# Differential attention between two expert layers: values split over four places of a batch, merge and xn two tiles apart, difference ahead of xn's remainder, the second map's factor on GpSimd

## The reference

```python
x = x + 0.5 * ffn(layernorm(x))      # 8 experts, top 2, hidden 512, then a layer norm of its own
x = x + attn(layernorm(x))
x = x + 0.5 * ffn(layernorm(x))

def attn(x):                          # scale = 128 ** -0.25
    a1 = softmax((x Wq1) (x Wk1)^T * scale)
    a2 = softmax((x Wq2) (x Wk2)^T * scale)
    diff = a1 - lam_full * a2         # lam_full: one number from four vectors
    out = diff @ (x Wv)
    return out / sqrt(mean(out ** 2) + 1e-5) * 0.2
```

## Time and profile before

| | |
|---|---|
| median of 3 runs | 728.55 us (727.17 to 728.67) |
| the profiled execution's own time | 725.22 us |
| its span | 723.5 us |
| mean granted TensorE clock | 0.911 |
| busy in the span: PE, DVE, ACT, POOL | 575.7, 517.6, 413.1, 335.3 us |
| busy from 256 to 502 us (attention): PE, DVE, ACT, POOL | 206.89, 211.63, 162.94, 102.02 us of 246.00 |

### The profile page before, as it was taken

The page is one execution under the profiler, slowest core; times in us unless marked ns, Lnnn a source line. Parts: engine busy times, 40 slices in busy tenths (PEclk is TensorE's granted clock), DMA queues, the critical chain, the costliest instruction groups (busy, mean ns, idle before and its releaser), DMA issues.

```text
span 723.5 us, 16279 instructions
## 1 busy us (share of the span) xinstructions
PE 575.7 (80%) x3864; PEld 500.8 (69%) x3864; DVE 517.6 (72%) x1672; ACT 413.1 (57%) x1103; POOL 335.3 (46%) x394
## 2 busy tenths in 40 slices
PE   1745399999799877897988789776999997999800
PEld 1734399999798856566675657654689897998800
DVE  5645657866578689799789967967266874688747
ACT  3354156666365638657767676565376563777621
POOL 6357035430546303533652164273377677456513
PEclk9965589999999999999999899898899998999955
DMA  8512134422443200000010000020313232521051
GB/s 272 154 45 78 44 86 115 113 63 76 118 106 84 56 1 15 23 22 1 26 34 2 0 30 31 0 75 18 71 54 96 77 88 75 193 75 44 26 174 58
DMA packets 53675, 49.17 MB, mean 68 GB/s; under 512 B 9862, under 2 KB 45874, under 8 KB 53072
## 3 DMA queue, kind: packets, MB, share of 16 engines
q1 hardware_dynamic: 44736, 31.25, 15.7%
q0 software_dynamic: 8640, 16.87, 7.5%
q10 hardware_dynamic: 208, 0.02, 0.0%
HBM read 25.99 MB, written 23.02 MB: 68 GB/s over the span
## 4 chain that ended last, share of the span: by engine, by line
PE 51%; DVE 25%; issue 8%; ACT 7%; POOL 6%; DMA 2%; DVEq 0%; ACTq 0%; POOLq 0%; SPq 0%
PE banks L847 18%; PE banks L857 17%; DVE nb L1419 5%; POOL zb L438 4%; PE banks L926 3%; PE banks L824 2%; PE banks L839 2%; DVE scratch L1430 2%; PE banks L780 2%; PE banks L782 1%; PE banks L781 1%; DVE st_r L1072 1%; PE banks L815 1%; DVE st_x L1072 1%; ACT rowbuf L535 1%
## 5 line engine op out<-in xcount | busy, mean ns | idle before, releaser
L847 PE MATMUL banks<-scratch 128*128 128x128 f32 x1248 | 171.5, 282 | 9.8 <-DVE scratch L1210 6.5
L857 PE MATMUL banks<-blocks,scratch 128*128 x1248 | 167.3, 278 | 0.4 <-ACT scratch L585 0.3
L847 PEld LDWEIGHTS banks<-scratch 128*128 128x128 f32 x1248 | 155.7, 196 | 15.2 <-issue 8.8
L857 PEld LDWEIGHTS banks<-blocks,scratch 128*128 128x128 f32 x1248 | 154.2, 194 | 0.7 <-issue 0.7
L1217 DVE TENSOR_SCALAR scratch<-banks,blocks 128x128 f32<-128x128 f32 x312 | 95.1, 346 | 46.7 <-PE banks L847 45.9
L427 POOL DMA_INDIRECT rows<-rowbuf,slot x96 | 96.3, 1003 | 46.4 <-issue 38.8
L572 ACT ACTIVATE scratch<-banks 128x128 f32<-128x128 f32 x156 | 43.2, 277 | 122.9 <-PE banks L839 116.1
L641 ACT ACTIVATE scratch<-banks,nb 128x1024 f32<-128x1024 f32 x64 | 71.2, 1114 | 68.3 <-DVE nb L1419 68.2
L585 ACT ACTIVATE scratch<-banks,blocks 128x128 f32<-128x128 f32 x312 | 97.7, 363 | 17.4 <-PE banks L847 15.9
L449 POOL DMA_INDIRECT results<-scratch x78 | 78.0, 1000 | 46.2 <-DVE scratch L1225 26.9
L438 POOL DMA_INDIRECT zb<-yrows,slot x64 | 67.2, 1049 | 62.1 <-DMA yrows<-scratch 25.3
(11 more groups left out here) (180 smaller groups left out, 876.8 us busy)
## 6 DMA issues: line engine op xcount, KB each, us to landing
scratch<-rows SPq DMA_DIRECT2D x156, 64.5 KB, 1.9
yrows<-scratch SPq DMA_DIRECT2D x78, 64.0 KB, 1.7
rows<-padrows SPq DMA_DIRECT2D x34, 64.5 KB
x<-in_L_attn_x_dram SPq DMA_DIRECT2D x4, 512.0 KB, 6.0
scratch<-in_L_ffn_W_dram SPq DMA_DIRECT2D x1, 2048.0 KB, 20.2
out_dram<-x SPq DMA_DIRECT2D x4, 512.0 KB, 5.9
rows<-rowbuf,slot POOLq DMA_INDIRECT x96
results<-scratch POOLq DMA_INDIRECT x78, 2.3
```

Source lines behind the costliest of these rows:

```text
L847: ins = pe.matmul(hT_at(T, c), staged(T, c), xT_of(T), start=True, stop=True)
L857: ins = pe.matmul(y_at(T), hT_of(T, c), blocks[:, W2_AT + c * D:][:, bass.ds(at, D)], start=(c == 0), stop=(c == FC - 1))
```

## The change

Nothing is computed otherwise than before, except that `1 / l2` is now a power of -1 on POOL. The edits are:

1. The factor `cc` moves from DVE (two instructions in each of 32 differences) to POOL: `ratio(b, i)` waits for both exponentials of tile i, takes `l2 ** -1`, and multiplies by `l1` and `-lambda`. DVE's `difference` now waits for `cc_ready`. To fit `ratio` in, POOL's gathers and scatters are cut into runs of 2 to 4 between the tiles.
2. `values` of a batch stand at four places: the first group's halves at tile 6 and behind `turn_xn`, the second group's halves at tiles 1 and 2 of the next batch; `multiply_Wv` of it moves to tile 3. The last batch keeps its places.
3. At the joint, PE has `values`' half and one `turn_rows` ahead of `multiply_M`, and `multiply_Wv` and the other `turn_rows` behind it; ACT's `o_copy` and a `copy_tgtT` move behind the last tile.
4. DVE's `merge_add` is at tile 3 and `x_stats` of xn stays at tile 5; `add_values` and its `x_stats` move from tile 3 to 4 (batches 1 and 2), `place` from tile 4 to 6 (batch 2). On ACT, `normalise` of `sum_r`, `make_rows` and `make_xn` are each done in one piece, no longer in two.
5. On DVE `difference(6)` is ahead of `xnT_rest`.

```diff
@@ -177,6 +177,7 @@
...
         found_rows = sem("found_rows")
+        cc_ready = sem("cc_ready")
         hT_first, w1_first, w1_rest = sem("hT_first"), sem("w1_first"), sem("w1_rest")
...
@@ -281,6 +282,10 @@
...
             return 0 if b == BATCHES - 1 else 2
+
+        def place_tile(b):
+
+            return 2 if b == BATCHES - 1 else 6
...
@@ -475,29 +481,37 @@
...
+            def ratio(b, i):
+
+                c = slice(i, i + 1)
+                wait_apart(pool, (p_ready, 2 * (TB * b + i) + 2))
+                steps.then(pool.tensor_tensor(cc[:, c], l2[:, c], minus[:, :], ALU.pow))
+                pool.tensor_scalar(cc[:, c], cc[:, c], l1[:, c], nlam[:, 0:1], ALU.mult, ALU.mult).then_inc(cc_ready, 1)
+
             n = BATCHES + 2
...
                 last, after = b > 0, b < BATCHES - 1
-                if b == BATCHES - 1:
-                    scatter(1, b - 3, range(10, PAIRS))
-                if after:
-                    rstd(n)
-                    n += 1
-                if last:
-                    value_scale(b - 1, 1)
-                    rstd(n)
-                    n += 1
-                if after:
-                    if b < 2:
-                        gather(b + 2, range(4))
-                    rstd(n)
-                    n += 1
-                if b < 2:
-                    gather(b + 2, range(4, PAIRS))
-                if b == 2:
-                    scatter(1, b - 2, range(10))
-                if b == BATCHES - 1:
-                    scatter(1, b - 2)
+                for i in range(TB):
+                    ratio(b, i)
+                    if after and i == 1:
+                        rstd(n)
+                        n += 1
+                    if last and i == 2 + after:
+                        value_scale(b - 1, 1)
+                    if last and i == 3 + after:
+                        rstd(n)
+                        n += 1
+                    if after and i == 5:
+                        rstd(n)
+                        n += 1
+                    if b < 2 and 1 <= i:
+                        gather(b + 2, range(16 * (i - 1) // 7, 16 * i // 7))
+                    if b == 2 and i >= 6:
+                        scatter(1, 0, range(3 * (i - 6), 3 * (i - 5)))
+                    if b == 3 and i < 3:
+                        scatter(1, 0, ((6, 7, 8), (9, 10, 11), (12, 13, 14, 15))[i])
+                    if b == 3 and i >= 4:
+                        scatter(1, 1, range(4 * (i - 4), 4 * (i - 3)))
                 value_scale(b, 0)
...
@@ -650,43 +664,40 @@
...
                             act.wait_ge(y_written[r], sent(SLOTS, r))
-                    if last and i == 2:
+                    if last and not after and i == 2:
                         o_copy(b - 1, 1)
                     if i == TB - 1:
-                        if last and after:
-                            copy_tgtT(a, 0)
-                        if after:
-                            o_copy(b, 0)
                         dT_copy(b, i - 2)
...
                             copy_tgtT(a, 1)
-                        if after:
-                            make_xn(b + 1, n + after + last, halves_of(1))
                     probabilities(i, 0)
...
                         dT_copy(b - 1, TB - 1)
-                    if last and i == 2:
+                    if last and i == 2 + after:
                         squares(b - 1, 1)
...
                         dT_copy(b, i - 2)
+                    if last and after and i == 2:
+                        o_copy(b - 1, 1)
                     if b > 1 and i == 1:
...
                         gap(a - 1)
-                    if after and i in (2, 3):
-                        ins = normalise(lambda j: sum_r[:, j * D:(j + 1) * D], sum_r, n, halves_of(i - 2))
-                        if i == 3:
-                            ins.then_inc(scaled, 1)
-                    if last and after and i in (4, 5):
-                        make_rows(1, b - 1, n + after, halves_of(i - 4))
+                    if after and i == 2:
+                        normalise(lambda j: sum_r[:, j * D:(j + 1) * D], sum_r, n).then_inc(scaled, 1)
+                    if last and after and i == 5:
+                        make_rows(1, b - 1, n + after)
                     if last and not after and i == 4:
...
                     if after and i == 6:
-                        make_xn(b + 1, n + after + last, halves_of(0))
+                        make_xn(b + 1, n + after + last)
                 if after:
+                    o_copy(b, 0)
+                    if last:
+                        copy_tgtT(a, 0)
                     copy_xm(b + 1)
...
@@ -948,8 +959,9 @@
...
                         values(b - 1, 1, 0)
+                    if last and i == 1 + after:
                         values(b - 1, 1, 1)
-                    if last and i == 2:
+                    if last and i == 2 + after:
                         multiply_Wv(b - 1, 1)
...
@@ -959,21 +971,22 @@
...
                         values(b, 0, 0)
-                        if after:
-                            values(b, 0, 1)
-                    if last and i == 6:
-                        turn_rows(a, int(not after))
+                    if last and not after and i == 6:
+                        turn_rows(a, 1)
                 if after:
                     turn_xn(b + 1)
+                    values(b, 0, 1)
                 if last and after:
-                    turn_rows(a, 1)
+                    turn_rows(a, 0)
                 if not after:
...
                     prefix(a)
-                multiply_Wv(b, 0)
                 if after:
                     multiply_M(b + 1)
+                multiply_Wv(b, 0)
+                if last and after:
+                    turn_rows(a, 1)
                 turn(b, TB - 2)
...
@@ -1421,11 +1434,9 @@
...
                     c = slice(i, i + 1)
-                    dve.wait_ge(p_ready, 2 * (TB * b + i) + 2)
+                    dve.wait_ge(cc_ready, TB * b + i + 1)
                     if i % QG == QG - 1:
                         dve.reciprocal(r1[:, i - QG + 1:i + 1], l1[:, i - QG + 1:i + 1])
-                    steps.then(dve.reciprocal(r2[:, c], l2[:, c]))
-                    steps.then(dve.tensor_scalar(cc[:, c], l1[:, c], r2[:, c], nlam[:, 0:1], ALU.mult, ALU.mult))
                     pp = p1[(TB * b + i) % 3]
...
@@ -1433,10 +1444,10 @@
...
                     maxima(i)
+                    if i:
+                        difference(i - 1)
                     if after and i == TB - 1:
                         xnT_rest(b + 1)
-                    if i:
-                        difference(i - 1)
                     if not after and i == TB - 1:
...
@@ -1452,16 +1463,17 @@
...
                         at_once(choose(a - 1))
-                    if last and i == 3:
+                    if after and i == 3:
+                        merge_add(b + 1)
+                    if last and i == 3 + after:
                         add_values(b - 1, 1)
...
                         n += 1
-                    if b > 1 and i == choose_tile(b) + 2:
+                    if b > 1 and i == place_tile(b):
                         at_once(place(a - 1, b - 2))
...
                     if after and i == 5:
-                        merge_add(b + 1)
                         x_stats(b + 1, n)
```

More of the change, by code:

```diff
@@ L156, in macaron_kernel @@
         l1, l2 = sb("l1", TB), sb("l2", TB)
-        r1, r2, cc = sb("r1", TB), sb("r2", TB), sb("cc", TB)
+        r1, cc = sb("r1", TB), sb("cc", TB)
         oT = [t[:, 0:QG * P] for t in dT]
@@ L392, in _ @@
             pool.memset(nhalf[:, :], -0.5)
+            pool.memset(minus[:, :], -1.0)
             pool.memset(onesE[:, :], 1.0)
```

2 lines of the change are left out of this document (1 added, 1 removed).

## The result

The changed kernel took 722.40 us (median of 15 runs, 720.19 to 726.50), the kernel before, run beside it, 727.08 us (15 runs, 722.46 to 728.67). The ratio is 0.9942, with a 95% interval of 0.9923 to 0.9960: 4.7 us faster by the medians. Medians are over all executions; single ones of some 3176 us, far outside all others (one of after_again, one of the kernel before on the slower chip), are left out of the ratios. The profiled execution of the changed kernel is its longest, 726.50 us, with a span of 724.8 us and a mean granted clock of 0.901; its other runs were at up to 0.914. So its span must not be held against the 723.5 us of before; stages and single rows can be.

A forecast was written before the change was run, and what follows sets the result against it. DVE was taken to bound loaded tiles, a loop bare ones, an ACT and PE chain the joints. Batch gains 1.35, 0.15, 3.05 and 0.95 make 5.5 us, less 1.8 for the clock: 3.7, median 724.8 us, range 719.5 to 730.

The forecast's parts named there:

- the clock's term: Batches 1 and 2: PE idling before tile 6's scores may lower its clock; 1.8 us taken off the gain.
- waits for POOL of over 1 us: Sign against the forecast: DVE was to wait only a few tenths for the factor, at tile 2 of batches 0 and 1.
- What bounds it: Attention: DVE ends loaded tiles, a 4.15 us loop of maxima, exp and scores bare ones, an ACT and PE chain the joints.
- Factor on GpSimd: Each of 32 differences loses 0.50 us on DVE; a ratio on POOL takes about 1.0 us, hidden unless POOL is late.
- The factor of tile 2 late by 0.2: Batches 0 and 1: factor ready 6.7 us after tile 2 starts, when DVE asks; 0 to 0.6 us lost, 0.2 taken.
- rival 2: Factor comes late behind POOL's gathers, with 1.5 us a ratio: 1.7 us lost, 726.5 us; chance 0.16.
- Place hidden, 3.2: Batch 2: place moves from full tile 4 into DVE's wait before tile 7's maxima, hiding 3.2 us.
- The joint gets longer: Tile 6 to next batch's first maxima: 0.85 us longer in batch 0, 1.15 in batches 1 and 2, plus 0.5 chain shift there.
- Halving the values buys nothing there: At the joint, tile 7's scores don't move, since turn(5) waits for ACT's copy of tile 4: no gain from halving.
- T + 7.1: Start of tile 7's maxima, T being tile 6's: said to stay unchanged, or T + 7.6 in batches 1 and 2.
- Rival 3: Joint runs at the lower clock after PE idles before turn(5): 6.5 us lost for one joint, 731.3 us; chance 0.12.
- Rival 4: A power on POOL holds up DVE's two-input SBUF instructions, 0.53 us each about 13 times: 7.0 us, 731.8; chance 0.03.

The follow-up runs named there:

- after_again: The changed kernel run once more, unedited: 722.82 us, ratio 0.9932 of the kernel before.
- p_again: Second run of the changed kernel with POOL's gathers of batches 0 and 1 kept away from tiles 1, 4 and 5: 719.84 us, ratio 0.9921.
- p_place_4: Changed kernel with POOL's gathers moved, plus place of batch 2 back at tile 4: 723.82 us, ratio 0.9976.
- b_joint_alone: The kernel before with only the changed kernel's joint (halved values, multiply_M first, o_copy last): 805.06 us on the slower chip, ratio 0.9960.
- factor_alone: The kernel before with only the factor on POOL and its gathers and scatters in short runs: 724.87 us, ratio 0.9953.
- q_and_logits: Changed kernel with POOL's gathers moved, last batch's values split, add_values ahead of reading logits: 774.22 us on the slower chip (0.9593), 715.18 us elsewhere (0.9852).

## Why the prediction was right, and which steps of it were not

The forecast was a gain of 3.7 us and a time of 724.8; the medians show a gain of 4.7 us, in the second measurement 4.0 (by its ratio 4.9), and 722.4 us lies inside the range. Of the 2.4 us between 724.8 and 722.4, 1.5 come from the kernel before, whose median over 15 runs is 727.08 and not the 728.55 of three.

The total came out better than its terms, and that is in part luck. The four stretches should have gained 5.5 us before the clock's term; after_again shows 2.55, the first profile of the changed kernel a loss of 0.7. The waits for POOL and the late xn, some 4 us together (after_again against p_again), were not in the sum but for 0.4, and the 1.8 us set aside for the clock stood in for part of them. The prediction had also named waits for POOL of over 1 us as a sign of being wrong, and two of 1.16 and 1.46 us came: the time held, this part of the account didn't. Batch by batch, from the timelines (gain over the kernel before, in us; predicted before the term for the clock):

| batch | predicted | after_again | p_again (no waits for POOL) |
|---|---|---|---|
| 0: tiles / joint | 2.2 / -0.85 | 0.73 / -0.46 | 2.04 / -0.46 |
| 1: tiles / joint and shift | 1.8 / -1.65 | 1.06 / -2.94 | 2.16 / -1.26 |
| 2: tiles / joint and shift | 4.7 / -1.65 | 5.00 / -1.27 | 4.99 / -1.26 |
| 3 to tile 6 | 0.95 | 0.43 | 0.43 |
| sum | 5.5 | 2.55 | 6.64 |

- **What bounds it** was read rightly: DVE in the loaded tiles, the loop in bare ones (4.18 us after, 4.15 forecast), a chain at the joints.
- **Factor on GpSimd.** The 0.50 us per loaded tile and the 0.98 us of a ratio are as forecast. The four stretches of p_again are 6.9 us shorter than those of the kernel with the factor on DVE; by the terms it was 8.0 without waits. The 6.9 is rough, since p_again's clock was higher there (0.98 against 0.95).
- **The factor of tile 2 late by 0.2** was mis-sized: 1.16 and 1.46 us. The `rstd` was taken as 2.6 us, and was 3.6, since DVE's difference held up POOL's `nm`. The sum had no slack (6.7 against 6.7), so all of the 1.0 us more became a wait. That is rival 2's mechanism, at 2.6 us of extra waits instead of its 1.7, and not by its cause (a dearer power).
- **A step that was missing:** the `rstd` of xn is on POOL too, behind three gathers and the factor of tile 5. It made ACT wait 1.53 us (1.56 in after_again), and the joint behind batch 1 grew by 2.9 us instead of 1.65. With the gathers moved it grew by 1.26.
- **Place hidden, 3.2:** shown by p_place_4 (3.14 us in its tile, 4.0 by the medians).
- **The joint gets longer:** right in kind, 0.46 us where 0.85 stood, 1.27 where 1.15 + 0.5 stood.
- **"Halving the values buys nothing there"** is the step that failed outright. It was read off the kernel before, where ACT's copy was last; the same change takes the merge from tile 5, and then the whole values are last, by 2.4 and 2.7 us in the first two joints. Taking the new joint away costs 5.3 us, where the prediction makes it a gain of 3.15. The forecast didn't suffer, because T + 7.1 was nearly right for the kernel with both edits (7.1, 7.5, 7.5 in p_again): the edit alone was judged wrongly, the pair rightly, and that is luck.
- **The clock, 1.8 us:** between two executions of the changed kernel it made 3.25 us in attention, so 1.8 is of the right size for one execution; as a cost of the change against the kernel before it isn't shown, since that one has such places too (a granted clock of 0.96 over the stretches, as after_again). Rival 3, a whole joint at the lower clock at 6.5 us, wasn't seen in the changed kernel; the joint behind batch 2 of its first profile lost 1.3 us by slow scores (21.65 against 20.33), and b_joint_alone shows a joint that begins so.
- **Rival 4** said that POOL would hold up DVE. It was the other way round. The Trainium skill's page SBUF — State Buffer, "Who interferes with whom", calls the shared pair of ports an exclusive lock between the two engines; with `nm` ending as DVE's two-input instruction ends, this trace agrees with that in DVE's favour. I had looked for the rule in one direction only. In the direction that rival 4 feared the traces still don't show it: in p_again a difference began 0.7 us into a power, and both took their usual time (POOL, then DVE):

```profile
348.17 1.67 POOL L423 TENSOR_TENSOR rs<-rs,nhalf 128x8 f32<-128x8 f32 x1
```
```profile
348.87 1.27 DVE L1441 SCALAR_TENSOR_TENSOR scratch<-scratch,cc 128x1024 f32<-128x1024 f32 x1
```

## What to carry to other kernels

An instruction on an idle engine isn't free because its own length fits: add up all that stands ahead of it in that engine's queue, with the lengths that these have beside the other engine's work, and look also at the older steps that now stand behind it. When several edits meet in one place, ask of each what is last there once the others are made; the kernel before can't answer that. And a long wait of the bounding engine that stood in the profile all along (here 4.02 us in the last batch, 3.42 in the kernel before) gave 3.3 us in its batch, while both variants of the joint that had just been tuned lost.

## What the runs showed of the hardware

- A DVE `scalar_tensor_tensor` with two inputs in SBUF holds up small POOL instructions: 0.20 us became 1.21 (275.33) and 1.19, a power of 8 columns 1.67 became 2.45 (358.75), one of 4 columns 1.02 became 1.87 in factor_alone (336.10), and the first of two gathers 1.08 became 2.09 (281.02). A POOL `tensor_scalar` that began 0.05 us into a difference kept its 0.27 us (358.40), so not every one is held. In the table of groups such an instruction shows only as a raised mean (0.99 us for `nm`). The other way round nothing was held up: the 32 differences of the changed kernel took 1.25 to 1.31 us each.
- A power on POOL of one column took 0.59 us, of four 1.02, of eight 1.67.
- The first product of tile 6's scores in batch 2 stands behind an idle time of PE of 3.08 us in both p_again (410.32) and the changed kernel (414.95); there it ran at full clock (0.50 us, the next 0.39), here at the 1.2 GHz level (0.79, the next 0.63). The length of the wait alone doesn't tell.
- One program's runs can fall into two groups by their mean clock (0.897 to 0.900 and 0.908 to 0.912), 7 us apart, so a profile of one of them says little on the median.
- One chip of those used took longer for both kernels that also ran elsewhere, and not by the same share: the kernel before went from 727.5 to 807.6 us (11%), at a mean clock of 0.87 instead of 0.91, the kernel of q_and_logits from 715.2 to 774.2 us (8%), at 0.88 to 0.89 instead of 0.91. The ratio of the two was 0.959 there and 0.985 elsewhere.
